# A pipelined attention and feed-forward kernel on one core: rotary tables renewed in two halves, the norm's mean computed by another instruction, and ScalarE's value copy moved in two of every four steps

## The chip, the cores and the metric

The kernel runs on one core of one Trainium2 chip. The metric is the device time of one execution in microseconds, the median over several runs. Before the change three runs gave 3952.9, 3954.86 and 3955.82 us.

## What is computed

`x` is 4 sequences of 1024 tokens of 128 channels, in float32. Two stacks of layers follow each other, each behind a layer norm and with a residual around it: eight blocks of linear attention with a feed-forward part, and then six layers of windowed attention with a feed-forward part. The change touches the second stack only (cut from the reference):

```
for i in range(DEPTH):                       # 6
    x = attn_layer(shift_tokens(x), Wqkv[i], q_scale[i], k_scale[i], Wo[i]) + x
    x = ffn_layer(shift_tokens(x), ln_g[i], ln_b[i], W1[i], b1[i], W2[i], b2[i]) + x
# attn_layer, 16 heads of 64:
q = l2norm(q) * qs;  k = l2norm(k) * ksc
q = q * cos * scale + rotate_half(q) * sin * scale
k = k * cos * inv + rotate_half(k) * sin * inv
out = local_attention(q, k, v)               # windows of 32, each sees itself and the one before
# ffn_layer:
mu = x.mean(-1, keepdims=True);  var = ((x - mu) ** 2).mean(-1, keepdims=True)
xn = (x - mu) / jnp.sqrt(var + 1e-05) * g + bln
a, gate = jnp.split(xn @ W1 + b1, 2, -1);  out = a * gelu(gate) @ W2 + b2
```

## The kernel before, in words

The program is written engine by engine: one loop over steps for each engine, in an order fixed by hand, with semaphores between them. Nothing schedules it afterwards. The first stack takes the first fifth of the time. The second works on tiles of 128 tokens: 6 layers of NT = 32 tiles are 192 tiles, and step `s` of every engine's loop holds pieces of several tiles. The products of tile s+1 are made, its squares and rotations taken (`square`, `sin_k`, `cos_k`, `sin_q`, `cos_q`, `sumsq`), tile s is turned and scored (`turned_k`, `turned_q`, `values`, `scores`, `masked`, `maxima`), tile s-1 goes through the exponentials (`exponents`, 16 heads, four at a time, one ScalarE instruction each), tile s-2 or s-3 through the attention product and the output.

The feed-forward part works on chunks of 4 tiles, so its pieces come round every four steps, and the steps differ by `s` mod 4. The text calls them:

- **turn step** (s mod 4 = 0, `stage(s, 8)`): the chunk is turned on TensorE, its mean and variance are taken on VectorE (`ff_stats`), rstd on GpSimd (`ff_rstd`), and ScalarE scales it (`ff_unit`, L980).
- **back step** (1, `stage(s, 9)`): turned back, ScalarE applies gain and bias (`ff_norm`, L988).
- **gate step** (2, `stage(s, 10)`): gates, values, gelu (`ff_gelu`, L994) and VectorE's `ff_hidden` (L1298).
- **down step** (3, `stage(s, 11)`): the second product and `ff_final` (L1305).

Lines that the text speaks of:

- ScalarE: L947 `turned_k` copies the turned keys, one in each step, and so marks the steps in the trace; L960 `exponents`; L952 `turned_q`; L975 `values` copies the value product out of PSUM and signals `v_r`; L936 `square`; L968 `outputs`.
- TensorE: L671 `product`, four matmuls, three times in a step (keys of tile s+1, queries of s+1, values of s); L724 `scores`; L743 `attend`; L703 turns. `keys_of` shares the two PSUM banks of the value product, and waits for `v_r` of the value copy:

```
                if t >= 2:
                    pe.wait_ge(v_r, t - 1)
```

- VectorE: L1185 `table_of` makes, for one tile position, the product of the rotary tables with the layer's scales (both in SBUF), 128x256 elements; it runs for the 8 positions of a sequence at the end of 8 steps before a new layer, 40 times in all. L1141 `tables_of` does it once for layer 0, in four instructions of 128x512. L1189 and L1196 (`cos`, `sin`) read these tables. L1217 `sumsq`. L1292 and L1293 in `ff_stats` write the negated mean and the variance plus epsilon. L1260 `masked` waits for all 16 exponentials of the tile before (`exp_r`), since it rewrites what they read. L1275 `turn_probs` transposes the probabilities; the next tile's exponentials wait for it (`pt_r`).
- GpSimd: L463 `add_k`, L468 `add_q`, L479 and L485 (`unit_k`, `unit_q`), L472 `probs_norm`, and L491 and L493 in `ff_rstd`; all read SBUF. Its order in a step: ff_rstd, add_q, unit_k, probs_norm, unit_q, add_k.

Of the kernel before, what the change touches and what calls it, by code (L numbers as in the profile page):

```python
# [14 lines left out]
ALU = mybir.AluOpType  # L15
# [4 lines left out]
P = 128  # L20
# [3 lines left out]
LAYERS, HEADS, DH, WIN = 6, 16, 64, 32  # L24
# [8 lines left out]
TS = SEQ // P  # L33
NT = NB * TS
# [9 lines left out]
EPS_PRE, EPS_A, EPS_F, EPS_Z = 1e-5, 1e-6, 1e-5, 1e-6  # L44
# [16 lines left out]
B_SC = B_WO + NP * D  # L61
# [10 lines left out]
def build(nc, xT, wa1, wa2, wb, wf, rot, mask, outT):  # L72
    with ExitStack() as ctx:
        def sb(name, shape):
            return ctx.enter_context(nc.sbuf_tensor(name, shape, F32))

        def sem(name):
            return ctx.enter_context(nc.semaphore(name))
# [13 lines left out]
        WB = sb("WB", [P, B_W])  # L92
# [3 lines left out]
        rotary = sb("rotary", [P, 4, TS, DH])  # L96
        tables = sb("tables", [P, 4, TS, DH])
# [4 lines left out]
        mv = sb("mv", [P, UT, 4, 2])  # L102
        ve = sb("ve", [P, UT, 4])
        rstd = sb("rstd", [P, UT, 4])
        mneg, shift = sb("mneg", [P, 4]), sb("shift", [P, 4])
# [17 lines left out]
        def carve(sizes):  # L123
# [32 lines left out]
        lq, lk, lv, lo, ls, lf = (sem(k) for k in ("wq_in", "wk_in", "wv_in", "wo_in", "scales_in", "wf_in"))  # L156
# [17 lines left out]
        fx_in, ft_mm, fst_r, frs_r, fn_r, fb_mm, xn_r, g_mm, a_mm, gate_r, hf_r, o_mm, fin_r = (sem(k) for k in (  # L174
            "ff_in", "ff_turned", "ff_stats", "ff_rstd", "ff_unit", "ff_back", "ff_normed", "gate_mm", "value_mm",
            "gate_ready", "hidden_ready", "ff_out", "ff_done"))
# [27 lines left out]
        def live(t):  # L204

            return 0 <= t < TILES

        def chunk(s, lag):

            return (s - lag) // PER if (s - lag) % PER == 0 and 0 <= s - lag < TILES else None  # L210

        def stage(s, lag):

            q = chunk(s + 1, lag)
            return q if q == FF - 1 else chunk(s, lag) if chunk(s, lag) != FF - 1 else None
# [29 lines left out]
        def heads(ap):  # L245
            return ap.rearrange("p (h d) -> p h d", d=DH)
# [597 lines left out]
        def _(act):  # L844
# [45 lines left out]
            def ff_gelu(c):  # L890
                act.wait_ge(f2_mm, MA * c + 4)
                act.activation(g2[c % 2], ps[:, F2_BANK, :], ACT.Gelu_apprx_tanh, bias=vec(c, A2_BF2))\
                    .then_inc(g2_r, 1)
# [39 lines left out]
            def square(t, src, half, mm, count):  # L933
                act.wait_ge(mm, t + 1)
                need(act, red_r, t)
                act.activation(sq[:, half], src.rearrange("p b c -> p (b c)"), ACT.Square).then_inc(count, 1)  # L936
# [7 lines left out]
            def turned_k(t):  # L944
                act.wait_ge(trk_mm, t + 1)
                act.wait_ge(shift_r, t + 1)
                act.activation(kT[:, :, WIN:WIN + P], s_ps.rearrange("p b (c t) -> p (b c) t", t=P),  # L947
                               ACT.Copy).then_inc(kT_r, 1)

            def turned_q(t):  # L950
                act.wait_ge(trq_mm, t + 1)
                act.activation(qTf, s_ps.rearrange("p b c -> p (b c)"), ACT.Copy).then_inc(qT_r, 1)  # L952

            def exponents(t, some):

                if some[0] == 0:
                    act.wait_ge(max_r, t + 1)
                    need(act, pt_r, t)
                for h in some:
                    i = act.activation(pe3[:, :, h, :], sc[:, 64 * h:64 * h + 64].rearrange("p (k q) -> p k q", k=2),  # L960
                                       ACT.Exp, bias=nmx[:, h:h + 1], accum_out=rs[:, h:h + 1])
                if some[-1] == HEADS - 1:
                    i.then_inc(exp_r, 1)

            def outputs(t):
                act.wait_ge(pv_mm, t + 1)
                need(act, wo_r, t)
                act.activation(OTf.rearrange("p (c r q) -> p r c q", r=2, q=WIN),  # L968
                               o_ps.rearrange("p r (c q) -> p r c q", q=WIN), ACT.Copy).then_inc(ot_r, 1)
# [28 lines left out]
            for s in range(-3, TILES + LAG):  # L998
                if live(s + 1):
                    square(s + 1, kv_ps, K, k_mm, sqk_r)  # L1000
                if live(s - 3):
                    outputs(s - 3)
                if live(s + 1):
                    square(s + 1, q_ps, Q, q_mm, sqq_r)
                if live(s):
                    turned_k(s)
                if live(s - 1):
                    exponents(s - 1, range(0, 4))
                    exponents(s - 1, range(4, 8))
                if live(s):  # L1010
                    turned_q(s)
                if live(s - 1):
                    exponents(s - 1, range(8, 12))
                if stage(s, 10) is not None:
                    ff_gelu(stage(s, 10), 0)
                    ff_gelu(stage(s, 10), 1)
                if live(s):
                    values(s)
                if stage(s, 9) is not None:
                    ff_norm(stage(s, 9))  # L1020
                if stage(s, 8) is not None:
                    ff_unit(stage(s, 8))
                if stage(s, 10) is not None:
                    ff_gelu(stage(s, 10), 2)
                if live(s - 1):
                    exponents(s - 1, range(12, 16))
                if 0 < s + 1 < TILES:
                    keys_on(s + 1)
# [3 lines left out]
        def _(dve):  # L1032
# [144 lines left out]
                    dve.wait_ge(loaded, 48)  # L1177
                    tables_of(0)

            def table_of(t):  # L1180

                if t % NT == 0:
                    dve.wait_ge(ls, 16 * (t // NT + 1))
                scales = WB[:, B_SC:B_SC + 4 * DH].rearrange("p (i d) -> p i d", i=4)
                dve.tensor_tensor(tables[:, :, t % TS, :], rotary[:, :, t % TS, :], scales, ALU.mult).then_inc(tab_r, 1)  # L1185

            def cos(t, src, half, o, count):
                w = tables[:, o, t % TS:t % TS + 1, :].to_broadcast([P, HEADS, DH])
# [27 lines left out]
            def sumsq(t):  # L1216
                dve.tensor_reduce(ssq[:, :], heads(sq), AX_X, ALU.add).then_inc(red_r, 1)  # L1217
# [64 lines left out]
            def ff_stats(q):  # L1282
                dve.wait_ge(ft_mm, q + 1)
                for j in range(PER):
                    o = dve.bn_stats(stats[:, 0, j, :], ps[:, FO_BANK(q), j * P:(j + 1) * P])
                o.then_inc(fst_r, 1)
                dve.wait_ge(fst_r, 3 * q + 1)
                for j in range(PER):
                    o = dve.bn_aggr(mv[:, 0, j, :], stats[:, 0, j, :])
                o.then_inc(fst_r, 1)  # L1290
                dve.wait_ge(fst_r, 3 * q + 2)
                dve.tensor_scalar(mneg[:, :], mv[:, 0, :, 0], -1.0, None, ALU.mult)  # L1292
                dve.tensor_scalar(ve[:, 0, :], mv[:, 0, :, 1], EPS_F, None, ALU.add).then_inc(fst_r, 1)  # L1293

            def ff_hidden(q, m):
                dve.wait_ge(gate_r, MF * q + m + 1)
# [18 lines left out]
            for s in range(-3, TILES + LAG):  # L1315
                if s > 0 and live(s + 1) and (s + 1) % NT == 0:
                    dve.wait_ge(tab_r, 4 + TS * ((s + 1) // NT))
                if live(s + 1):
                    sin_k(s + 1)
                if live(s - 2):  # L1320
                    turn_probs(s - 2)
                if live(s + 1):
                    cos_k(s + 1)
                if stage(s, 8) is not None:
                    ff_stats(stage(s, 8))
                if live(s + 1):
                    sin_q(s + 1)
                    cos_q(s + 1)
                    sumsq(s + 1)
                if stage(s, 10) is not None:  # L1330
                    ff_hidden(stage(s, 10), 0)
                if stage(s, 11) is not None:
                    ff_final(stage(s, 11))
                if stage(s, 10) is not None:
                    ff_hidden(stage(s, 10), 1)
                if live(s - 3):
                    residual(s - 3)
                if live(s + 1):
                    norms(s + 1)
                if stage(s, 10) is not None:  # L1340
                    ff_hidden(stage(s, 10), 2)
                if live(s):
                    masked(s)
                if live(s - 1):
                    inverse(s - 1)
                if live(s):
                    maxima(s)
                if live(s + 1 + TS) and (s + 1 + TS) // NT > (s + 1) // NT and s >= -1:
                    table_of(s + 1 + TS)
                q = stage(s, 12)  # L1350
                if q is not None and q >= FF - NT // PER:
                    final(q)
# [71 lines left out]
```

## Time and profile before

| | |
|---|---|
| median of 3 runs | 3954.86 us |
| the profiled execution, its own time | 3945.2 us |
| its span, first to last instruction | 3943.3 us |
| mean granted TensorE clock | 0.985 |
| PE (TensorE) busy | 3714.9 us, 94% |
| DVE (VectorE) busy | 3453.9 us, 88% |
| ACT (ScalarE) busy | 3279.6 us, 83% |
| POOL (GpSimd) busy | 2401.3 us, 61% |

The profile is one execution. Times in the trace are microseconds from the span's start. An engine's idle time before an instruction is put down to what released it; "issue" is time for which the profile shows no releaser.

### The profile page before, as it was taken

The page shows a single profiled execution, that of the slowest core. Times are in us where ns is not written, and L with a number is a line of the kernel's source. Part 1 is how long each engine was busy: PE and PEld are TensorE (multiplying, and loading weights), DVE is VectorE, ACT ScalarE, POOL GpSimd, SP SyncE. Part 2 cuts the span into 40 slices and gives each one's busy share as a digit, 9 for nine tenths or more (in the row PEclk, how much of TensorE's full clock was granted, in tenths as well). Part 3 has the DMA queues.
Part 4 walks back from the last instruction along what each step waited for, and adds up shares of the span by engine and source line. Part 5 has one row for each costly group of instructions (what it writes and reads, how often), then busy time and mean ns, then how long its engine had stood idle before and what let it go on. Part 6 is the DMA issues. An engine that isn't in the chain of part 4 may idle for free.

```text
span 3943.3 us, 124130 instructions
## 1 busy us (share of the span) xinstructions
PE 3714.9 (94%) x49248; PEld 2335.7 (59%) x49248; DVE 3453.9 (88%) x7052; ACT 3279.6 (83%) x9259; POOL 2401.3 (61%) x1476
## 2 busy tenths in 40 slices
PE   6999999978999999999999999999999999999997
PEld 3444444445666666666666666666666666666664
DVE  7999999968889898889989899898988989888894
ACT  4999999956888788888888888888888888888885
POOL 2444444447767676766767666676666766676672
PEclk8999999989999999999999999999999999999998
DMA  1000001002223233232232233332323223232222
GB/s 38 9 9 9 9 9 50 1 3 61 82 82 87 77 87 83 81 92 81 82 85 81 82 85 88 83 83 80 87 81 85 81 79 95 80 85 82 79 81 57
DMA packets 129889, 263.10 MB, mean 67 GB/s; under 512 B 34976, under 2 KB 36768, under 8 KB 129056
## 3 DMA queue, kind: packets, MB, share of 16 engines
q1 hardware_dynamic: 129312, 255.16, 23.1%
q8 instruction: 392, 6.42, 0.7%
q14 instruction: 185, 1.52, 0.1%
HBM read 26.43 MB, written 2.10 MB: 7 GB/s over the span
## 4 chain that ended last, share of the span: by engine, by line
PE 42%; DVE 24%; ACT 20%; issue 7%; POOL 3%; DMA 1%; SPq 1%; ACTq 0%; DVEq 0%; POOLq 0%
ACT arena L960 10%; PE ps L671 9%; PE ps L608 6%; PE ps L603 5%; PE ps L743 4%; PE ps L547 4%; DVE arena L1196 4%; DVE arena L1189 3%; DVE arena L1275 3%; PE ps L515 3%; DVE ssq L1217 3%; DVE arena L1260 2%; ACT arena L952 2%; ACT arena L947 2%; PE ps L791 2%
## 5 line engine op out<-in xcount | busy, mean ns | idle before, releaser
L960 ACT ACTIVATE arena<-arena,nmx 128x64 f32<-128x64 f32 x3072 | 1024.3, 339 | 55.3 <-DVE arena L1275 53.0
L479 POOL TENSOR_TENSOR arena<-arena,rinv 128x1024 f32<-128x1024 f32 x192 | 365.6, 1904 | 615.1 <-DVE rinv L1248 615.1
L671 PE MATMUL ps<-WB,arena 128*128 128x512 f32 x1152 | 566.9, 615 | 35.1 <-ACT arena L975 28.4
L671 PE MATMUL ps<-WN,arena 128*128 128x512 f32 x1152 | 562.4, 611 | 34.5 <-ACT arena L975 29.3
L960 ACT ACTIVATION_READ_ACCUMULATOR arena<-arena,nmx 128x1 f32 x3072 | 589.6, 192 | 0.0
L936 ACT ACTIVATE arena<-ps 128x1024 f32<-128x1024 f32 x384 | 392.2, 1022 | 227.0 <-PE ps L671 221.6
L463 POOL TENSOR_TENSOR arena<-arena 128x1024 f32<-128x1024 f32 x192 | 454.2, 2366 | 193.7 <-DVE arena L1189 178.4
L1196 DVE TENSOR_TENSOR arena<-ps,tables 128x512 f32<-128x512 f32 x768 | 489.9, 677 | 17.0 <-ACT arena L936 16.6
L468 POOL TENSOR_TENSOR arena<-arena 128x1024 f32<-128x1024 f32 x192 | 453.9, 2364 | 51.0 <-DVE arena L1189 46.9
L743 PEld LDWEIGHTS ps<-arena 128*64 128x64 f32 x12288 | 377.0, 138 | 164.9 <-issue 139.0
L1189 DVE TENSOR_TENSOR arena<-ps,tables 128x1024 f32<-128x1024 f32 x384 | 459.0, 1195 | 0.0
L1217 DVE TENSOR_REDUCE ssq<-arena 128x32 f32<-128x2048 f32 x192 | 435.0, 2266 | 0.0
L703 PEld LDWEIGHTS ps<-ident,arena 128*128 128x128 f32 x3072 | 354.1, 142 | 121.4 <-issue 98.8
L743 PE MATMUL ps<-arena 128*64 128x64 f32 x12288 | 402.6, 224 | 16.9 <-DMA arena<-arena 11.6
L472 POOL TENSOR_TENSOR arena<-arena,rr 128x1024 f32<-128x1024 f32 x192 | 368.0, 1917 | 82.3 <-DVE rr L1269 82.1
L703 PE MATMUL ps<-ident,arena 128*128 128x128 f32 x3072 | 401.8, 274 | 15.6 <-POOL arena L485 5.5
L724 PEld LDWEIGHTS ps<-arena 64*32 64x32 f32 x24576 | 266.1, 105 | 201.4 <-issue 199.0
L752 PE MATMUL ps<-arena,WB 128*128 128x128 f32 x3072 | 377.3, 276 | 1.4 <-ACT arena L968 1.1
L485 POOL TENSOR_TENSOR arena<-arena,rinv 128x1024 f32<-128x1024 f32 x192 | 375.2, 1954 | 0.0
L752 PEld LDWEIGHTS ps<-arena,WB 128*128 128x128 f32 x3072 | 360.8, 193 | 1.8 <-ACT arena L968 1.3
L420 POOL TENSOR_TENSOR rstdA<-veA,power 128x4 f32<-128x4 f32 x128 | 129.7, 1013 | 374.7 <-DVE veA L1135 374.7
L724 PE MATMUL ps<-arena 64*32 64x64 f32 x24576 | 300.1, 225 | 47.0 <-issue 24.1
(111 smaller groups left out, 7040.7 us busy)
## 6 DMA issues: line engine op xcount, KB each, us to landing
arena<-arena SPq DMA_DIRECT2D x1536, 64.0 KB, 2.0
arena<-arena SPq DMA_DIRECT2D x192, 384.0 KB, 3.4
arena<-arena SPq DMA_DIRECT2D x192, 128.0 KB, 3.5
arena<-X SPq DMA_DIRECT2D x96, 128.0 KB, 3.0
arena<-Y SPq DMA_DIRECT2D x96, 128.0 KB, 3.1
WB<-wb SPq DMA_DIRECT2D x15, 512.0 KB, 5.1
arena<-wa SPq DMA_DIRECT2D x8, 581.0 KB, 4.1
WN<-wb SPq DMA_DIRECT2D x9, 512.0 KB, 5.0
```

Source lines behind the costliest of these rows:

```text
L463: pool.tensor_tensor(tu[:, K], t1[:, K], t2[:, K], ALU.add).then_inc(addk_r, 1)
L468: pool.tensor_tensor(tu[:, Q], t1[:, Q], t2[:, Q], ALU.add).then_inc(addq_r, 1)
L671: i = pe.matmul(banks[:, c, :], x, W[:, w * INNER + c * COL:w * INNER + (c + 1) * COL], start=True, stop=True)
L703: i = pe.transpose(s_ps[:, j // 4, (j % 4) * P:(j % 4 + 1) * P], src[:, j * P:(j + 1) * P], ident[:, :])
L724: i = pe.matmul(s_ps[WIN * w:WIN * (w + 1), a, c * 64:c * 64 + 64], qT[r, c, WIN * w:WIN * (w + 1)], kT[r, c, WIN * w:WIN * (w + 2)], star ...
L743: i = pe.matmul(o_ps[64 * a:64 * a + 64, side, c * 64:(c + 1) * 64], vv[t % RING][:, side, h * DH:(h + 1) * DH], pw[:, side, :, a, c, :], ...
L752: i = pe.matmul(o_ps[:, 0, 0:P], WB[:, B_WO + c * D:B_WO + (c + 1) * D], OT[:, c, :], start=(c == 0), stop=(c == NP - 1))
L936: act.activation(sq[:, half], src.rearrange("p b c -> p (b c)"), ACT.Square).then_inc(count, 1)
L960: i = act.activation(pe3[:, :, h, :], sc[:, 64 * h:64 * h + 64].rearrange("p (k q) -> p k q", k=2), ACT.Exp, bias=nmx[:, h:h + 1], accum_o ...
L1189: dve.tensor_tensor(heads(t1[:, half]), src.rearrange("p b (h d) -> p (b h) d", d=DH), w, ALU.mult)\
L1196: k = dve.tensor_tensor(heads(t2[:, half])[:, :, here], src.rearrange("p b (h d) -> p (b h) d", d=DH)[:, :, there], w, ALU.mult)
L1217: dve.tensor_reduce(ssq[:, :], heads(sq), AX_X, ALU.add).then_inc(red_r, 1)
```

## The change

Three edits, the constants and all data unchanged.

```
@@ scalar engine, step s
                 if live(s):
                     turned_q(s)
+                early = stage(s, 8) is not None or stage(s, 9) is not None
+                if live(s) and early:
+                    values(s)
                 if live(s - 1):
                     exponents(s - 1, range(8, 12))
                 if stage(s, 10) is not None:
                     ff_gelu(stage(s, 10), 0)
                     ff_gelu(stage(s, 10), 1)
-                if live(s):
+                if live(s) and not early:
                     values(s)
@@ vector engine
-            def table_of(t):
-
-                if t % NT == 0:
-                    dve.wait_ge(ls, 16 * (t // NT + 1))
-                scales = WB[:, B_SC:B_SC + 4 * DH].rearrange("p (i d) -> p i d", i=4)
-                dve.tensor_tensor(tables[:, :, t % TS, :], rotary[:, :, t % TS, :], scales, ALU.mult).then_inc(tab_r, 1)
+            def tables_half(l, half, t):
+
+                dve.wait_ge(ls, 16 * (l + 1))
+                dve.wait_ge(rotq_r, 2 * (t + 1))
+                some = slice(TS // 2 * half, TS // 2 * (half + 1))
+                for i in range(4):
+                    w = WB[:, B_SC + i * DH:B_SC + (i + 1) * DH].unsqueeze(1).to_broadcast([P, TS // 2, DH])
+                    dve.tensor_tensor(tables[:, i, some, :], rotary[:, i, some, :], w, ALU.mult).then_inc(tab_r, 1)
@@ ff_stats
-                dve.tensor_scalar(mneg[:, :], mv[:, 0, :, 0], -1.0, None, ALU.mult)
-                dve.tensor_scalar(ve[:, 0, :], mv[:, 0, :, 1], EPS_F, None, ALU.add).then_inc(fst_r, 1)
+                mean, var = mv[:, 0, :, 0], mv[:, 0, :, 1]
+                dve.scalar_tensor_tensor(mneg[:, :], mean, -2.0, mean, ALU.mult, ALU.add)
+                dve.scalar_tensor_tensor(ve[:, 0, :], var, EPS_F, var, ALU.add, ALU.max).then_inc(fst_r, 1)
@@ vector engine, step s, behind sumsq(s + 1)
+                l = (s + 1) // NT + 1
+                if s > 0 and l < LAYERS and (s + 1) % NT in (NT - 5, NT - 1):
+                    tables_half(l, (s + 1) % NT == NT - 1, s + 1)
@@ vector engine, step s, behind maxima(s)
-                if live(s + 1 + TS) and (s + 1 + TS) // NT > (s + 1) // NT and s >= -1:
-                    table_of(s + 1 + TS)
```

The order on ScalarE, a back step before the change (arena is the one large SBUF tensor that holds most buffers, ps is PSUM, WF the feed-forward weights):

```order
L947 ACTIVATE arena<-ps 128x8x128
L960 ACTIVATE arena,rs<-arena,nmx 128x2x32 x8
L952 ACTIVATE arena<-ps 128x1024
L960 ACTIVATE arena,rs<-arena,nmx 128x2x32 x4
L975 ACTIVATE arena<-ps 128x1024
L988 ACTIVATE arena<-ps,WF 128x512
L960 ACTIVATE arena,rs<-arena,nmx 128x2x32 x4
```

The same on ScalarE with the change:

```order
L947 ACTIVATE arena<-ps 128x8x128
L960 ACTIVATE arena,rs<-arena,nmx 128x2x32 x8
L952 ACTIVATE arena<-ps 128x1024
L975 ACTIVATE arena<-ps 128x1024
L960 ACTIVATE arena,rs<-arena,nmx 128x2x32 x4
L988 ACTIVATE arena<-ps,WF 128x512
L960 ACTIVATE arena,rs<-arena,nmx 128x2x32 x4
```

The value copy (L975) now stands ahead of the third four exponentials; in turn steps it is the same with L980 in place of L988, and gate and down steps keep their order.

The order on VectorE before, from the end of one of the 40 steps with a table to its next rotations:

```order
L1260 TENSOR_TENSOR arena<-ps,maskt 128x1024
L1269 RECIPROCAL rr<-rs 128x16
L1265 TENSOR_REDUCE nmx<-arena 128x16
L1185 TENSOR_TENSOR tables<-rotary,WB 128x4x64
L1196 TENSOR_TENSOR arena<-ps,tables 128x16x32 x2
L1275 STREAM_TRANSPOSE arena<-arena 128x1024
```

And on VectorE with the change, in one of the 10 gate steps that now renew half of the tables (L1194 is `cos_q`, L1222 `sumsq`, L1304 `ff_hidden`, L1285 `residual`, L1226 `clamp`, by the new line numbers):

```order
L1194 TENSOR_TENSOR arena<-ps,tables 128x1024
L1222 TENSOR_REDUCE ssq<-arena 128x32
L1190 TENSOR_TENSOR tables<-rotary,WB 128x256 x4
L1304 SCALAR_TENSOR_TENSOR arena<-ps,WF,arena 128x512 x2
L1285 TENSOR_TENSOR Y<-ps,X 128x128
L1226 TENSOR_SCALAR ssc<-ssq 128x32
```

The table products left the end of eight consecutive steps and stand, four together, between `sumsq` and `ff_hidden` of two gate steps in each layer. TensorE's, GpSimd's and SyncE's orders are unchanged.

## Rows read from the trace of the kernel before

**Rows 1.** Page: busy us of each engine, share of the span, instructions.

```profile
PE 3714.9 (94%) x49248; PEld 2335.7 (59%) x49248; DVE 3453.9 (88%) x7052; ACT 3279.6 (83%) x9259; POOL 2401.3 (61%) x1476
```

**Rows 2.** Chain of waits in order of time: start us, us, what. A turn step.

```profile
2020.30 0.92 ACT arena L975
...
2021.35 1.95 PE ps L671 x4
```

**Rows 3.** Waits: engine and line, what released it, us in total, times, longest.

```profile
DVE arena L1298 <- ACT arena L994: 137.1, 81, 3.2
...
PE ps L671 <- ACT arena L975: 57.7, 89, 0.8
```

**Rows 4.** Timeline of a turn step: start us, us, engine, line, [idle before <-releaser].

```profile
2014.96 2.37 POOL L463 TENSOR_TENSOR arena<-arena 128x1024 f32<-128x1024 f32 x1 [0.61 <-DVE arena L1189]
...
2016.14 1.21 DVE L1292 TENSOR_SCALAR mneg<-mv 128x4 f32<-128x4 f32 x1
...
2017.26 1.88 PE L671 MATMUL ps<-WB,arena 128*128 128x512 f32 x4
...
2017.97 1.00 ACT L952 ACTIVATE arena<-ps 128x1024 f32<-128x1024 f32 x1
...
2023.71 0.21 ACT L960 ACTIVATION_READ_ACCUMULATOR arena<-arena,nmx 128x1 f32 x1
...
2024.02 1.23 DVE L1260 TENSOR_TENSOR arena<-ps,maskt 128x1024 f32<-128x1024 f32 x1
...
2027.91 1.25 DVE L1275 STREAM_TRANSPOSE arena<-arena 128x1024 f32<-128x1024 f32 x1 [0.22 <-POOL arena L472]
...
2029.25 0.35 ACT L960 ACTIVATE arena<-arena,nmx 128x64 f32<-128x64 f32 x1
```

**Rows 5.** Timeline of the back step that follows.

```profile
2031.04 1.88 PE L671 MATMUL ps<-WB,arena 128*128 128x512 f32 x4
...
2031.92 1.00 ACT L952 ACTIVATE arena<-ps 128x1024 f32<-128x1024 f32 x1
...
2033.07 1.59 PE L724 MATMUL ps<-arena 64*32 64x64 f32 x128
...
2035.30 1.96 PE L671 MATMUL ps<-WB,arena 128*128 128x512 f32 x4 [0.65 <-ACT arena L975]
...
2036.95 0.19 ACT L960 ACTIVATION_READ_ACCUMULATOR arena<-arena,nmx 128x1 f32 x1
...
2042.15 1.02 ACT L947 ACTIVATE arena<-ps 128x1024 f32<-128x1024 f32 x1
```

**Rows 6.** Timeline of the gate step that follows.

```profile
2045.44 2.27 DVE L1217 TENSOR_REDUCE ssq<-arena 128x32 f32<-128x2048 f32 x1
...
2045.60 2.37 POOL L468 TENSOR_TENSOR arena<-arena 128x1024 f32<-128x1024 f32 x1
...
2050.06 0.75 DVE L1298 SCALAR_TENSOR_TENSOR arena<-ps,WF,arena 128x512 f32<-128x512 f32 x1 [2.36 <-ACT arena L994]
```

**Rows 7.** Groups of instructions: line, engine, shapes, count, busy us, mean ns, idle before.

```profile
L1185 DVE TENSOR_TENSOR tables<-rotary,WB 128x256 f32<-128x256 f32 x40 | 62.1, 1553 | 0.0
L1292 DVE TENSOR_SCALAR mneg<-mv 128x4 f32<-128x4 f32 x48 | 53.4, 1113 | 1.7
...
L1134 DVE TENSOR_SCALAR mnegA<-mvA 128x4 f32<-128x4 f32 x128 | 21.8, 170 | 4.4
```

**Rows 8.** One line's instructions: count, ns least/median/most, first and last start.

```profile
L1141 DVE TENSOR_TENSOR tables<-rotary,WB x4: 677/678/1687, 838.1 to 840.9; 128x512 f32<-128x512 f32 x4
```

**Rows 9.** One line's instructions, the first squaring of the root steps.

```profile
L1236 DVE TENSOR_TENSOR nwt<-rinv x192: 191/192/2371, 897.0 to 3868.9; 128x32 f32<-128x32 f32 x192
```

**Rows 10.** Timeline of L947: starts of steps 47, 55 and 63.

```profile
1624.23 1.02 ACT L947 ACTIVATE arena<-ps 128x1024 f32<-128x1024 f32 x1
...
1746.37 1.02 ACT L947 ACTIVATE arena<-ps 128x1024 f32<-128x1024 f32 x1
...
1875.51 1.02 ACT L947 ACTIVATE arena<-ps 128x1024 f32<-128x1024 f32 x1
```

## The prediction

> **What bounds the kernel now.** I read four views. The page first [rows 1]: TensorE is busy 94% of the span, VectorE 88%, ScalarE 83%; no engine has much air, and an average over steps of four kinds does not say which one sets the end. So next the chain of waits, in order of time [rows 2]: what to see there is a hand-over in the turn step, where ScalarE's value copy L975 ends and TensorE's key products L671 start. Then the waits [rows 3]: TensorE stood 57.7 us before L671 for that copy, in 89 steps, never above 0.8 us; and VectorE stood 137.1 us before L1298 for the gelus, 2.9 us for each of the 48 chunks, all in gate steps. Last the timelines of a turn, a back and a gate step [rows 4 to 6], from which the arithmetic is made.
>
> A loop over two engines limits a step besides TensorE. The last exponential of a tile ends at 2023.92 (L960 at 2023.71, [rows 4]), `masked` L1260 can start 0.1 us later, then follow the reciprocal, `maxima`, `sin_k` and the transpose L1275, and only when that has ended, at 2029.16, may the next tile's exponentials begin: they do at 2029.25. So in the turn step this loop and not TensorE releases ScalarE.
>
> **1. Tables.** Removed: 40 instructions L1185 of 1553 ns, 62.1 us [rows 7]. Each stands at a step's end, in that loop, between `maxima` and `sin_k`. What they cost the end is read from the step marks: from step 47 to 55 no table is made, 122.14 us; from 55 to 63 the eight tables of a layer are made, 129.14 us [rows 10], the same eight kinds of steps. That is 7.0 us for eight, of 12.4 us of instructions. For five layer changes: 35 us gained.
>
> Added: 10 times four instructions of 128x256, with the same 40 x 256 elements. Why did the old ones take 1553 ns? The same product over 512 elements took 678 ns in its median, 1687 at most [rows 8], and 4 elements take 170 ns (L1134, [rows 7]). The line through the two, 1 ns for each element, gives 0.42 us for 256; that is what I take. Bounds: 0.34 (half of 678) and 1.55 (as before). What makes the difference is GpSimd working at the same time. In the gate step `sumsq` ends at 2047.71 and GpSimd's L468 at 2047.97 [rows 6]; behind it GpSimd has nothing until VectorE's root steps. If the first instruction waits for 2047.97, four end at 2047.97 + 4 x 0.42 = 2049.65, and L1298 is to start at 2050.06, 0.65 earlier once edit 3 acts: 2049.41. Not hidden: 0.2 us, 10 times, 2 us. The new wait for `rotq_r` is for an instruction ahead of `sumsq` on the same engine, and costs nothing; behind it queue `ff_hidden` and the root steps, for which GpSimd waits. With the upper bound the four take 6.2 us, 4.5 beyond the cover left, 45 us in all: no gain from this edit but a loss of 10. Tables: 33 us gained (between +10 lost and 35 gained).
>
> **2. The mean.** L1292 writes 128x4 values and takes 1113 ns in its mean [rows 7], the same form in the first stack 170 ns (L1134). The timeline says why: it starts at 2016.14 and ends at 2017.35, when GpSimd's L463 ends, at 2017.33 [rows 4]. If the new form escapes, 48 x 0.94 = 45 us of VectorE go, all in turn steps. Does it? It now reads `mean` twice, as two SBUF inputs. The nearest row is L1236, which also takes one SBUF tensor twice: 192 ns, but 2371 once [rows 9], when it began beside GpSimd's L468. So an instruction with two SBUF inputs can be held too, and I expect L1292's successor to take about 1.1 us still.
>
> The Trainium skill ("SBUF — State Buffer", section "Who interferes with whom") says the same more sharply: a VectorE instruction with two SBUF inputs contends with a GpSimd instruction that reads SBUF, and the later one is blocked entirely. By it the edit removes nothing; that the old form is held agrees with the trace, for the new form no row of this kernel exists.
>
> Either way the sum hardly moves: L1260 starts 0.1 us after the last exponential, so a VectorE that is 1 us earlier at that point waits instead. I take 0 (between 0 and 45).
>
> **3. The value copy.** *Back step* [rows 5]: the value product ends at 2032.92, `turned_q` at 2032.92, so L975 can follow at once; its successors in PSUM, the keys, then wait only for TensorE. The scores end at 2034.66, and TensorE's keys follow at once, 0.65 us earlier than 2035.30. Behind them on TensorE stand `attend`, the queries and the turn of the keys, each without another wait that lasts as long (L988, for which `attend` waits, keeps its place behind 12 exponentials and one copy), so L947 of the next step comes at 2041.5 instead of 2042.15. The loop allows it: the last exponential keeps its end at 2037.14, and 5.11 us later (the time from 2023.92 to 2029.25, less the 0.22 us that L1275 stood for GpSimd) is 2042.25; ScalarE is ready about 0.9 us behind the start of L947 (its 1.02 us less the overlap seen between neighbours), at 2042.4. Of the 57.7 us, back steps hold the share 0.65 / (0.65 + 0.76) = 27 us.
>
> *Turn step* [rows 4]: the value product ends at 2019.14, later than `turned_q` at 2018.97. ScalarE, which goes on about 0.1 us before 2018.97 now, stands until 2019.18: 0.3 us in which the exponentials behind it would have run. They end 0.3 later, `masked` starts 0.3 later, and the 0.22 us for GpSimd before L1275 swallow most of that: 0.08 us are left. TensorE's keys come 0.76 us earlier, but the next exponentials are released by the loop, so this is not gained. Cost: 48 x 0.08 = 4 us, taken off what the back steps win, 27 - 4 = 23 us. (Bounds: 57.7 if all of the wait pays, and -14 if 0.3 us were lost in each turn step and nothing won.)
>
> **Sum.** 33 + 0 + 23 = 56 us off the profiled execution's 3945.2: 3889. The median of the runs shown is 9.7 above that execution, so the median forecast is 3899.
>
> **The rivals.**
> - *The value copy pays nothing* (0.15). For it: the loop is only 0.2 us behind in the back step, and TensorE has gaps of its own inside the scores that no reordering moves. Against: 0.65 us is a wait that ends last in 44 steps. Tables alone: 3955 - 33 = 3922.
> - *The mean escapes, and VectorE was the bound in turn steps* (0.09). Then turn steps gain as well, all of the 57.7: 3955 - 33 - 58 = 3864. Against: L1236's 2371, and L1260's place behind the exponentials.
> - *The tables are held as before* (0.06): halves at 1.55 us each, 10 us lost, 23 gained by the copy: 3942. Against: GpSimd is idle from 2047.97 on.
> - *Slower: ScalarE stands before the value copy* (0.06). The copy now has 4 exponentials behind it, which the loop needs. If the value product came as late as 1 us behind `turned_q` (in the turn step it is 0.17 behind), 96 steps would lose nearly 1 us each: 96 - 33 = 63 slower, 4018. It decides from (33 + 2)/96 = 0.36 us of lateness on. Against: in the back step it is not late at all.
> - *Nothing to be seen* (0.04): table gain given back by waits elsewhere in the 8 steps; 3955.
>
> **How the numbers follow.** The forecast has 0.60: 3899, with 3884 to 3914 for the bounds of its terms. About 0.2% (8 us) is what a measurement of this kernel can tell from no change. Faster by more: 0.60 + 0.15 + 0.09 + 0.05 of the third rival, 0.88 after rounding down; within: 0.05; slower: 0.07. The range for 8 in 10 takes in the tables-alone case and, half, the case of the mean: 3868 to 3927.
>
> **What would show it.** The table group: 40 instructions near 0.4 us, and steps 55 to 63 within 1 us of steps 47 to 55. The successor of L1292: near 1.1 us if it is held, 0.17 if it escapes. L671's wait for L975 gone in turn and back steps; back steps 0.5 us shorter or more, turn steps no shorter. VectorE's idle time before L1298 smaller by 1.6 us in ten gate steps. I am wrong if turn steps get shorter (the loop was not the bound), if L975 waits over 0.3 us for the value product, or if the halves take over 1 us each.

## The result, and the profile after

Four runs of the changed kernel gave 3901.35 us (3897.38 to 3905.21); four of the kernel before, one of them new, 3955.34 us. The ratio is 0.9871, with a 95% interval of 0.9856 to 0.9886: 1.3% less, 45 to 57 us. The profiled execution took 3905.21 us, its span 3903.4 us against 3943.3; it is the slowest of the four, so the two traces stand 40 us apart where the medians stand 54. Of all the executions below one, of the run with the mean alone, was slow (6865.9 us, at a granted clock of 0.83), and it is left out of that run's ratio.

The page of the changed kernel, busy time by engine, which answers to [rows 1]:

```profile
PE 3706.9 (95%) x49248; PEld 2330.6 (60%) x49248; DVE 3410.1 (87%) x7052; ACT 3278.4 (84%) x9259; POOL 2392.7 (61%) x1476
```

VectorE is 43.8 us less busy. Its groups of instructions, which answer to [rows 7] (line, shapes, count, busy us, mean ns, idle before):

```profile
L1298 DVE SCALAR_TENSOR_TENSOR mneg<-mv 128x4 f32<-128x4 f32 x48 | 51.8, 1078 | 1.6
...
L1190 DVE TENSOR_TENSOR tables<-rotary,WB 128x256 f32<-128x256 f32 x40 | 16.3, 464 | 0.0
```

The 40 table products went from 1553 to 464 ns each; the mean in its new form takes 1078 ns, as good as the 1113 of the old. The waits, which answer to [rows 3]:

```profile
DVE arena L1304 <- ACT arena L994: 116.0, 74, 3.2
DVE arena L1265 <- ACT arena L960: 106.2, 146, 3.2
...
PE ps L743 <- DMA arena<-arena: 38.8, 55, 6.3
```

VectorE's wait for the gelus, the cover of the tables, fell from 137.1 to 116.0 us. TensorE's wait for the value copy, 57.7 us before, is 4.3 us (6 times). The third of these lines is new in size: `attend` L743 is put down as waiting 38.8 us for DMAs, 11.6 us before. The timeline of one back step shows such a wait (start us, us, engine, line, idle before):

```profile
2391.27 1.00 ACT L952 ACTIVATE arena<-ps 128x1024 f32<-128x1024 f32 x1
2392.17 1.00 ACT L975 ACTIVATE arena<-ps 128x1024 f32<-128x1024 f32 x1
...
2394.04 1.98 PE L671 MATMUL ps<-WN,arena 128*128 128x512 f32 x4
...
2397.26 2.08 PE L743 MATMUL ps<-arena 128*64 128x64 f32 x64 [1.24 <-DMA arena<-arena]
```

The copy follows `turned_q` at once and the keys start without a wait, as forecast. But behind them `attend` stands 1.24 us. The chain of waits in order of time says for what:

```profile
2387.29 1.23 DVE arena L1280
...
2388.53 0.54 SPq L325
...
2389.12 0.59 SPq L326
...
2392.92 0.59 SPq L326
...
2394.19 3.04 DMA arena<-arena
...
2397.26 2.08 PE ps L743 x64
```

From the transpose's end at 2388.52 SyncE issues eight DMAs (`widen`, which spreads the probabilities over the wide buffer that `attend` reads), one every 0.63 us, until 2393.51; then they have to land. The last piece of the chain is named after L332, the DMA that SyncE issues next, but that one moves the values of a tile whose `attend` comes later; `attend` here waits for the last widening DMA, issued at 2392.92. From issue to landing that one took 4.2 us, where the median is 2.0:

```profile
L326 SPq DMA_DIRECT2D arena<-arena x4: 590/591/594, 2389.1 to 2392.9; - x4
...
DMA to landing us min/median/max: 2.0/2.0/4.2
```

In the trace fifteen of its sixteen parts have landed by 2394.90 and the last at 2397.12, and `attend` starts 0.14 us later. So it goes in 19 of 46 back steps (in 22 before the change): the last part lands over 1 us behind the others. Of the 20.2 us that `attend` stands in back steps, 16.1 fall in those 19. What holds the last part up isn't shown.

Not all of the 38.8 us is a wait for these DMAs. In turn steps it looks like this:

```profile
2380.77 1.48 ACT L980 ACTIVATE arena<-ps,shift,rstd 128x128 f32<-128x128 f32 x4
2382.30 1.30 PEld L743 LDWEIGHTS ps<-arena 128*64 128x64 f32 x42 [1.28 <-ACT arena L980]
2382.30 1.39 PE L743 MATMUL ps<-arena 128*64 128x64 f32 x40 [0.45 <-DMA arena<-arena]
```

`attend` starts 0.05 us behind the end of ScalarE's L980, for which it waits too, and the widening DMAs had landed about 2.8 us earlier; the line that names a DMA names the wrong one of several waits. There are 25 such stands of about 0.45 us in the row, 11 us, and all but one of the rest, 26.6 us in 29 steps, end with the last widening DMA.

Where the marks of the steps stand now:

```profile
1622.35 0.35 ACT L960 ACTIVATE arena<-arena,nmx 128x64 f32<-128x64 f32 x1
...
1743.04 0.35 ACT L960 ACTIVATE arena<-arena,nmx 128x64 f32<-128x64 f32 x1
...
1864.25 0.35 ACT L960 ACTIVATE arena<-arena,nmx 128x64 f32<-128x64 f32 x1
```

These are the first exponentials of steps 47, 55 and 63: 120.7 us without tables, 121.2 us with the two halves. The table stretch costs 0.5 us more than the one ahead of it, where it cost 8.3 before.

### The profile page after: what moved, and what is told of

It is laid out like the page before. It is cut to its first block, busy times and chain, and to the rows that moved or that the text cites. A ratio compares the mean times of both kernels' runs of the same rounds, so it can differ in the third digit from the quotient of the medians.

```text
span 3903.4 us, 124140 instructions
## 1 busy us (share of the span) xinstructions
PE 3706.9 (95%) x49248; PEld 2330.6 (60%) x49248; DVE 3410.1 (87%) x7052; ACT 3278.4 (84%) x9259; POOL 2392.7 (61%) x1476
## 4 chain that ended last, share of the span: by engine, by line
PE 66%; ACT 15%; DVE 7%; issue 5%; SPq 3%; DMA 3%; POOL 1%; ACTq 0%; DVEq 0%; POOLq 0%
PE ps L671 18%; ACT arena L960 8%; PE ps L743 8%; PE ps L608 6%; PE ps L603 5%; PE ps L752 5%; PE ps L703 5%; PE ps L547 4%; PE ps L515 3%; PE ps L724 3%; PE ps L806 3%; DMA arena<-arena 2%; PE ps L791 2%; PE ps L799 2%; SPq L325 2%
## 5 line engine op out<-in xcount | busy, mean ns | idle before, releaser
L479 POOL TENSOR_TENSOR arena<-arena,rinv 128x1024 f32<-128x1024 f32 x192 | 365.3, 1902 | 613.1 <-DVE rinv L1253 613.1
L671 PE MATMUL ps<-WB,arena 128*128 128x512 f32 x1152 | 573.6, 622 | 7.6 <-ACT arena L975 4.3
L671 PE MATMUL ps<-WN,arena 128*128 128x512 f32 x1152 | 562.6, 611 | 3.0 <-DVE arena L1194 3.0
L743 PEld LDWEIGHTS ps<-arena 128*64 128x64 f32 x12288 | 378.1, 139 | 199.8 <-issue 133.9
L468 POOL TENSOR_TENSOR arena<-arena 128x1024 f32<-128x1024 f32 x192 | 453.7, 2363 | 53.2 <-DVE arena L1194 47.5
L1194 DVE TENSOR_TENSOR arena<-ps,tables 128x1024 f32<-128x1024 f32 x384 | 459.3, 1196 | 0.0
L743 PE MATMUL ps<-arena 128*64 128x64 f32 x12288 | 404.1, 224 | 46.1 <-DMA arena<-arena 38.8
L1222 DVE TENSOR_REDUCE ssq<-arena 128x32 f32<-128x2048 f32 x192 | 435.1, 2266 | 0.0
L472 POOL TENSOR_TENSOR arena<-arena,rr 128x1024 f32<-128x1024 f32 x192 | 367.8, 1916 | 86.6 <-DVE rr L1274 86.3
L485 POOL TENSOR_TENSOR arena<-arena,rinv 128x1024 f32<-128x1024 f32 x192 | 367.7, 1915 | 0.0
```

Source lines behind the costliest of these rows:

```text
L468: pool.tensor_tensor(tu[:, Q], t1[:, Q], t2[:, Q], ALU.add).then_inc(addq_r, 1)
L671: i = pe.matmul(banks[:, c, :], x, W[:, w * INNER + c * COL:w * INNER + (c + 1) * COL], start=True, stop=True)
L743: i = pe.matmul(o_ps[64 * a:64 * a + 64, side, c * 64:(c + 1) * 64], vv[t % RING][:, side, h * DH:(h + 1) * DH], pw[:, side, :, a, c, :], ...
L1194: dve.tensor_tensor(heads(t1[:, half]), src.rearrange("p b (h d) -> p (b h) d", d=DH), w, ALU.mult)\
```

## The experiments

Each run is compared by ratio with the kernel before on the same chip; in us it is said of 3955, to stand beside 3901. The sets were run at other times and on several chips; their medians for the kernel before are 3948 to 3949, not 3955, and which of the two makes that isn't known.

A step is measured below from its first exponential to the next step's, as the median over the steps without tables. In the kernel before a turn step is 13.94 us and a back step 13.80; in the changed kernel 13.94 and 13.75.

**Each edit alone.** Tables only is the changed kernel with these lines undone:

```
-                early = stage(s, 8) is not None or stage(s, 9) is not None
+                early = False
-                dve.scalar_tensor_tensor(mneg[:, :], mean, -2.0, mean, ALU.mult, ALU.add)
-                dve.scalar_tensor_tensor(ve[:, 0, :], var, EPS_F, var, ALU.add, ALU.max).then_inc(fst_r, 1)
+                dve.tensor_scalar(mneg[:, :], mv[:, 0, :, 0], -1.0, None, ALU.mult)
+                dve.tensor_scalar(ve[:, 0, :], mv[:, 0, :, 1], EPS_F, None, ALU.add).then_inc(fst_r, 1)
```

> The changed kernel with the copy and the mean as before, so that the tables in halves stand alone. Theory (tables carry most of the gain: the first exponentials of turn, back and gate steps come 2.5, 0.5 and 1.3 us sooner in each of 10 steps with tables, about 41 us): 3915 us against 3955, and back and turn steps without tables as before. Rival (the copy carries most): the tables alone give 28 us or less, 3927 or more.

Measured: 3900.66 us, ratio 0.9887 (0.9868 to 0.9906), 45 us of gain. The tables carry most of it; the rival is out. In the profiled executions 39 of the 45 us between this kernel and the one before lie in the five stretches with tables. Their instructions take 467 ns as in the changed kernel.

Copy only is the kernel before with the first hunk of the change.

> The kernel before with only the value copy moved, in turn and back steps. Theory: the wait of L671 for L975 (57.7 us before) is gone, but TensorE's attend now waits for the widening DMAs (38.8 us in the changed kernel, 11.7 before), and turn steps stay bound by the exponentials' loop: 8 to 20 us gained, 3940. The forecast's own figure was 23 us, 3932. Rival (the copy pays all it removes): over 40 us, below 3915.

Measured: 3939.0 us, ratio 0.998 (0.9969 to 0.9992), 8 us of gain (3 to 12). The forecast's figure of 23 is out, and so is the rival. The typical turn and back step are 13.94 and 13.76 us. L671's wait for the copy is 4.3 us, and the wait for DMAs appears here too, without the other edits:

```profile
PE ps L743 <- DMA arena<-arena: 49.0, 71, 6.6
```

Mean only is the kernel before with the last two `+` lines of `ff_stats`.

> The kernel before with only the mean and the variance in the new form. Theory (two SBUF inputs are held as long as the old form, 1.08 us in the changed kernel): within 3 us of before, 3955, its group near 1.1 us in the mean. Rival (the form is worth something, by the shorter hold in some steps): 5 us or more gained.

Measured: 3948.75 us, ratio 0.9998 (0.9985 to 1.001): no effect that can be told from none.

```profile
L1293 DVE SCALAR_TENSOR_TENSOR mneg<-mv 128x4 f32<-128x4 f32 x48 | 52.9, 1102 | 1.6
```

The form is held as the old one was. The three ratios multiplied give 0.9865, the change 0.9871: as far as these intervals tell, the edits add up.

**The copy in back steps only**, with the tables and the old mean:

```
-                early = stage(s, 8) is not None or stage(s, 9) is not None
+                early = stage(s, 9) is not None
```

> The changed kernel with the copy moved in back steps only (turn steps as before) and the mean as before. Theory (the copy in turn steps delays ScalarE by 0.3 us and wins nothing, the back step alone wins): 3898, equal to the changed kernel's 3901 or 1 to 4 us faster. Rival (turn steps win too, since attend of the turn step starts 0.25 us sooner): 5 us or more slower than the changed kernel.

Measured: 3897.87 us, ratio 0.9874 (0.9856 to 0.9892), not to be told from the change's 0.9871. So the copy's move in turn steps is worth nothing that could be seen, as forecast (the forecast had it lose 4 us, which is below the noise).

**Half of the widening DMAs left out**, with the change and then with the tables alone. In `widen` (the counts that three waits ask for go down with it):

```
                     sp.dma_start(PTw[q, w % 2, here], pt[q, COL:2 * COL]).then_inc(wide_in, 16)
-                    sp.dma_start(PTw[o:o + WIN, w % 2, here], pt[q, 0:COL]).then_inc(wide_in, 16)
```

> The changed kernel with four of the eight widening DMAs of each tile left out (those of the window before are not brought into the wide buffer, so the attention product leaves them out), and its waits counted accordingly. Theory (attend waits for these DMAs since the keys come sooner, 38.8 us in 55 steps, and that is where the copy's gain went): that wait falls below 5 us and the time falls by 10 to 25 us below the changed kernel's 3901, to about 3885. Rival (the exponentials' loop takes the gain anyway): the wait goes, the time stays within 5 us of 3901.

> The tables in halves alone (value copy and mean as before), with the same four of eight widening DMAs left out: the control to the run with the copy. Theory (the DMAs matter only where the copy lets the keys come sooner, since the wait was 11.9 us in 12 steps without it): at most 10 us below the tables alone, 3890 to 3900, and so the copy is worth 15 us or more once the DMAs are short. Rival (fewer DMAs help whatever the order is): 20 us or more below the tables alone, 3880 or less, the copy still worth 8 or less.

Measured: with the copy 3874.88 us, ratio 0.9812 (0.9798 to 0.9827); without it 3897.45 us, ratio 0.9863 (0.985 to 0.9876). With the copy the time fell by 23 us below the change. In pairs: with all DMAs the copy takes the ratio from 0.9887 to 0.9871, 6 us (-3 to 16 by the two intervals); with half of them from 0.9863 to 0.9812, 20 us (12 to 28). The difference, 14 us, is thus known to some 12 us only. The steps tell it more sharply:

| | turn step, us | back step, us |
|---|---|---|
| tables only | 13.92 | 13.79 |
| the change | 13.94 | 13.75 |
| half of the DMAs, no copy | 13.93 | 13.79 |
| half of the DMAs, with the copy | 13.94 | 12.99 |

With all eight DMAs the copy's move leaves the typical back step as it was, with four it takes 0.8 us off it. Neither fewer DMAs alone nor the copy alone shortens it. (By ratio the run with half of the DMAs and no copy is 9 us below tables only, at the edge of what the intervals tell.) The 0.8 us would be 38 us in 48 back steps; the medians of the runs give 20, and where the rest goes isn't shown. The row of `attend` in the run with the copy:

```profile
PE ps L742 <- DMA arena<-arena: 12.5, 27, 0.6
```

That is not below 5, as was expected, but none of it is a wait for widening DMAs: all 27 are turn steps, where `attend` follows ScalarE's L979 (L980 elsewhere) and the widening DMAs landed some 5 us earlier. In back steps they land 3.4 us before `attend` starts, with no last part behind the others by more than 1 us.

**One exponential ahead of the copy in turn steps:**

```
+                lead = 1 if stage(s, 8) is not None else 0
+                if live(s - 1) and lead:
+                    exponents(s - 1, range(8, 8 + lead))
                 if live(s) and early:
                     values(s)
                 if live(s - 1):
-                    exponents(s - 1, range(8, 12))
+                    exponents(s - 1, range(8 + lead, 12))
```

> The changed kernel with one more head's exponential ahead of the value copy in turn steps, so that ScalarE does not stand 0.3 us for the value product. Theory (the loop from the last exponential to the next first one sets the turn step, and the stand is in it): turn steps 0.3 us shorter from first exponential to first exponential, 48 times, up to 14 us, 3890. Rival (something else, TensorE's attend behind L980 or the DMAs, sets the turn step): within 4 us of 3901.

Measured: 3896.06 us, ratio 0.9877 (0.9859 to 0.9894): not to be told from the change, where the theory's 14 us would have given 0.984. The timeline of a turn step tells why:

```profile
1454.36 1.22 DVE L1268 TENSOR_TENSOR arena<-ps,maskt 128x1024 f32<-128x1024 f32 x1
...
1458.24 1.25 DVE L1283 STREAM_TRANSPOSE arena<-arena 128x1024 f32<-128x1024 f32 x1 [0.21 <-POOL arena L472]
...
1454.43 1.90 POOL L479 TENSOR_TENSOR arena<-arena,rinv 128x1024 f32<-128x1024 f32 x1 [1.92 <-DVE rinv L1256]
1456.30 1.92 POOL L472 TENSOR_TENSOR arena<-arena,rr 128x1024 f32<-128x1024 f32 x1
```

Counted from the first exponential, the last one ends at 8.60 us (8.92 in the changed kernel) and `masked` starts at 8.70 (9.02), but the transpose starts at 12.58 (12.61): it now waits 0.21 us for GpSimd's L472, which stands behind L479, which waited for VectorE's root steps. The turn step is 13.93 us in its median, 13.94 in the changed kernel: a second chain, through the root steps and GpSimd, is as long as the first.

**The mean by a reduction.** First one of the two instructions, then both:

```
-                dve.scalar_tensor_tensor(mneg[:, :], mean, -2.0, mean, ALU.mult, ALU.add)
+                dve.tensor_reduce(mneg[:, :], mv[:, 0, :, 0:1], AX_X, ALU.max, negate=True)
...
+                dve.tensor_reduce(ve[:, 0, :], mv[:, 0, :, 1:2], AX_X, ALU.max).then_inc(fst_r, 1)
```

> The changed kernel with the negated mean written by a reduction over one element, one SBUF input, with the variance in its old form. Theory: this form is not held by GpSimd, its group falls from 1.08 us to under 0.25, VectorE is 0.8 us earlier in turn steps and then waits for ScalarE's last exponential, so the time stays within 4 us of 3901. Rival (VectorE's hold is worth time): 10 us or more gained. If the group stays near 1.1 us the hold is not a matter of the second input.

Measured: 3902.73 us, ratio 0.9881 (0.9865 to 0.9896). The reduction takes 157 ns, but the tensor_scalar behind it then takes the hold over:

```profile
L1298 DVE TENSOR_SCALAR ve<-mv 128x4 f32<-128x4 f32 x48 | 49.4, 1030 | 0.0
...
L1297 DVE TENSOR_REDUCE mneg<-mv 128x4 f32<-128x4 f32 x48 | 7.5, 157 | 1.6
```

VectorE was hardly sooner free, so this run says which form is held, not what the hold costs.

> The changed kernel with the negated mean and the variance both written by a reduction over one element, so that neither has a second SBUF input nor is a tensor_scalar; the epsilon is left out of the variance. In the run with one reduction the reduction took 157 ns and the tensor_scalar behind it 1030. Theory: both take under 0.2 us, VectorE waits longer for ScalarE's last exponential instead, the time within 5 us of 3901. Rival (VectorE's hold is worth time): 10 us or more gained.

Measured: 3884.48 us, ratio 0.9832 (0.9815 to 0.9848): 15 us below the change, with intervals that do not meet. So the theory's "within 5" is out, and the rival's number came. A turn step of this run:

```profile
1440.73 0.16 DVE L1297 TENSOR_REDUCE mneg<-mv 128x4 f32<-128x4 f32 x1
1440.81 0.15 DVE L1298 TENSOR_REDUCE ve<-mv 128x4 f32<-128x4 f32 x1
...
1448.93 1.23 DVE L1265 TENSOR_TENSOR arena<-ps,maskt 128x1024 f32<-128x1024 f32 x1 [1.35 <-ACT arena L960]
```

VectorE is 1 us earlier and waits that 1 us before `masked`: 1.36 us in its median, 0.32 in the changed kernel. The typical turn step is 13.94 us in both. So the theory holds for the typical step, and the gain isn't in it. TensorE stands now and then within the scores, 1 to 2.5 us with no releaser:

```profile
2088.95 0.30 PE L724 MATMUL ps<-arena 64*32 64x64 f32 x3 [2.38 <-issue]
2089.17 3.66 PE L671 MATMUL ps<-WB,arena 128*128 128x512 f32 x4
```

(These two lines are from the changed kernel.) Such stands over 0.8 us make 23.0 us in the changed kernel's trace (11 of them), and the nine groups of four matmuls that took over 2.5 us, where 1.95 is usual, another 13.6; with both reductions they are 12.3 us (6) and 2.2 (two groups). That is 22 of the 26 us between the two profiled executions, but these are single executions, one of them the slowest of its four; the other traces, all with the hold, have 14 to 23 us of such stands. Whether the missing hold has a part in there being fewer, or is worth time in some other way in the untypical steps, isn't settled: no run here changes the stands alone.

**The halves in the old place:** behind `maxima` in place of behind `sumsq`, in the same gate steps.

```
-                if s > 0 and l < LAYERS and (s + 1) % NT in (NT - 5, NT - 1):
-                    tables_half(l, (s + 1) % NT == NT - 1, s + 1)
...
                 if live(s):
                     maxima(s)
+                l = (s + 1) // NT + 1
+                if s > 0 and l < LAYERS and (s + 1) % NT in (NT - 5, NT - 1):
+                    tables_half(l, (s + 1) % NT == NT - 1, s + 1)
```

> The changed kernel with the halves behind the maxima of the same gate steps, where the old products stood, beside GpSimd's L472 and L485. Theory (the old products were slow because of their place, held by GpSimd): four take 4 to 6 us, in the exponentials' loop, 10 times 3 to 5 us in full: 3931 to 3951, most of the tables' gain lost. Rival (the form, four contiguous halves, is what made them fast): each stays near 0.46 us, 10 x 1.7 = 17 us lost, 3918.

Measured: 3942.34 us, ratio 0.9984 (0.9975 to 0.9993): 45 us slower than the change, the tables' gain given back whole.

```profile
L1190 DVE TENSOR_TENSOR tables<-rotary,WB 128x256 f32<-128x256 f32 x40 | 39.7, 1050 | 0.0
```

1050 ns is a mean of two kinds. One set of four, and GpSimd beside it:

```profile
1307.81 3.98 DVE L1190 TENSOR_TENSOR tables<-rotary,WB 128x256 f32<-128x256 f32 x4
...
1306.87 1.92 POOL L472 TENSOR_TENSOR arena<-arena,rr 128x1024 f32<-128x1024 f32 x1 [1.33 <-DVE rr L1274]
1308.74 2.08 POOL L485 TENSOR_TENSOR arena<-arena,rinv 128x1024 f32<-128x1024 f32 x1
```

The first two take 1.26 and 2.12 us and each ends 0.3 us behind GpSimd's L472 and L485; the last two, with GpSimd done, take 0.41 each. Behind `sumsq` the first takes 0.6, with the end of L468 beside it, and the other three 0.41. So the place makes them slow or fast and not the form: the old ones, 1.26 to 1.84 us, had GpSimd beside all of them. The four are 4 us in one piece, in the loop, 10 times: 40 us.

**Two versions against the DMA chain.** Two of the eight DMAs issued by GpSimd behind its second unit product (it is `widen`'s w = 3, with a semaphore of its own):

```
+                if live(s - 2):
+                    widen_last(s - 2)
                 if live(s + 1):
                     add_k(s + 1)
```

> The changed kernel with two of the eight widening DMAs issued by GpSimd, behind its second unit product, and six by SyncE, whose issue chain is 1.3 us shorter. Theory (attend waits for the last widening DMA): the wait of L743 for DMAs falls below 15 us and the time by 8 to 20 us, 3885. Rival (issuing them costs GpSimd more than its idle 0.6 us, or they land late): the same or slower than 3901.

Measured: 3892.23 us, ratio 0.9852 (0.9839 to 0.9866). `attend`'s wait for DMAs is put at 16.7 us, a little over what was expected, but none of it in back steps (the last tile apart): there the last widening DMA lands 2.1 us before `attend` starts. The time is 8 us below the change, with intervals that overlap (0.9856 to 0.9886). The back step fell to 13.30 us and the turn step rose to 14.33: most of what one wins the other gives back. Which of the products behind the two issues on GpSimd (0.58 and 0.50 us) makes the turn step longer isn't shown.

```
-                dve.transpose(pt, pe_).then_inc(pt_r, 1)
+                for k in (1, 0):
+                    dve.transpose(pt[:, k * COL:(k + 1) * COL], pe_[:, k * COL:(k + 1) * COL]).then_inc(pt_r, 1)
```

Here SyncE issues the four DMAs of the first half after the first transpose.

> The changed kernel with the transpose of the probabilities in two halves, so that the first four widening DMAs start 0.6 us sooner. Theory (the DMA chain bounds attend, VectorE's loop pays 0.07 us a step for the second instruction, 13 us at most): between 3885 and 3900. Rival (the loop pays more than the chain wins): 3905 to 3915.

Measured: 3893.27 us, ratio 0.9852 (0.9839 to 0.9866), the wait 28.4 us. Here too the back step is shorter, 13.28 us, and the turn step longer, 14.11. These two have the lowest ratios of the kernels that leave nothing out, but neither is set apart from the change with certainty.

## Why the prediction was right, and where it was not

The forecast was 3899 us, the measured 3901.35. That the sum came out so close is luck: two of its terms were wrong, and their errors, +12 and -15, stood against each other.

*Tables: 33 forecast, 45 measured (37 to 52), above the term's own upper bound of 35.* The mechanism was right: the new place is free of GpSimd's hold but for the end of L468 (0.42 us forecast for an instruction, 0.41 measured where GpSimd is idle, 0.464 in the mean; 1.05 in the old place), and it is covered by the wait for the gelus. The size was read at the wrong mark. The forecast took 7.0 us for eight tables from the starts of L947 [rows 10]. But the last table of the eight stands at the end of step 62, and delays the transpose and the exponentials of step 63, which start behind L947 of that step. The first exponentials of the same steps in the trace before:

```profile
1625.27 0.35 ACT L960 ACTIVATE arena<-arena,nmx 128x64 f32<-128x64 f32 x1
...
1747.40 0.35 ACT L960 ACTIVATE arena<-arena,nmx 128x64 f32<-128x64 f32 x1
...
1877.85 0.35 ACT L960 ACTIVATE arena<-arena,nmx 128x64 f32<-128x64 f32 x1 [1.32 <-DVE arena L1275]
```

130.45 against 122.13 us, 8.3 for this layer change. Over all five the stretches with tables are longer than those ahead of them by 42.8 us between first exponentials and by 35.9 between L947. The forecast had itself named that loop as the place. Nor did the halves cost the 2 us that were put down for them: in a gate step that has them L1304 still waits for the gelu.

```profile
1365.22 1.64 DVE L1190 TENSOR_TENSOR tables<-rotary,WB 128x256 f32<-128x256 f32 x4
1367.60 0.75 DVE L1304 SCALAR_TENSOR_TENSOR arena<-ps,WF,arena 128x512 f32<-128x512 f32 x1 [0.74 <-ACT arena L994]
```

*The value copy: 23 forecast, 8 measured alone (3 to 12), 6 on top of the tables (-3 to 16).* The step that failed is "each without another wait that lasts as long", of what stands behind the keys. `attend` had such a wait: for the widening DMAs. It hardly showed before (3.7 us in all back steps), since the last of these DMAs landed just before `attend` could start, 0.4 us in the median; with keys 0.65 us sooner it ends last. The forecast looked for such a wait on ScalarE (L988) and not on SyncE, whose eight issues are 5 us from the transpose's end, with a last part that in 19 of 46 back steps lands over 1 us late. Its sign "back steps 0.5 us shorter or more" did not come: 13.75 us for 13.80. With half of these DMAs left out the back step is 0.8 us shorter and the copy is worth 20 us (12 to 28), which takes in the 23.

*Turn steps win nothing:* right, the run with the copy in back steps only shows it. Of the reason, half: besides the loop of the exponentials there is the chain through root steps and GpSimd's L472, of equal length. ScalarE stood 0.21 us for the value product, of the 0.3 forecast. By the marks of L947 the turn step did get 0.28 us shorter (13.50 for 13.78), which the forecast had named as a sign against it, and the back step as much longer (14.32 for 14.02): only the mark between them moved. From first to first exponential the turn step stayed (13.94 in both).

*The mean: held, and 0:* right for the form as changed. L1236, a tensor_tensor with one tensor twice, was the right row. The Trainium skill ("SBUF — State Buffer", section "Who interferes with whom") lets a VectorE instruction with two SBUF inputs be blocked by a GpSimd instruction that reads SBUF, and says of a reduction that it never contends. The traces agree: in this place the scalar_tensor_tensor took 1.08 to 1.10 us and the reduction 0.157. The tensor_scalar, with one SBUF input, took 1.03 to 1.11, so it was held as well. That the sum would not move if the hold went was argued from the typical step and is true of that step; the run without any hold is 15 us faster all the same. Most of what its one trace shows of that are fewer stands of TensorE, and the cause is open.

Of the rivals, "the value copy pays nothing" came nearest to what was found: with the forecast's 33 for the tables it gives 3922, which is out, but with the 45 measured it gives 3910, and the change as a whole (45 to 57 us) hardly rules that out. It is the copy alone, 3 to 12 us, that does.

## What to carry to other kernels

Read what an instruction costs between two marks that lie behind it in the loop that it delays, not at the nearest convenient mark. When a wait is taken away, list for each instruction behind it every semaphore that it waits for, with the time at which each comes, the DMA issuer's queue included: the wait that ended just before the one removed shows almost nothing in the totals and is the next bound. Where an instruction waits for several things, a profile's row names one of them: check it against when the others came, as with the 0.45 us in turn steps that a DMA was named for and ScalarE's L980 made. Keep a VectorE product of two SBUF tensors away from GpSimd's work by its place: one of 128x256 cost 0.41 us where GpSimd was idle and 1.26 to 2.12 beside it. And a sum that comes out is no proof of its terms; the runs with one edit each are what showed these two wrong.

## What was not expected of the hardware

The hold passes on: with the mean written by a reduction (0.157 us) the tensor_scalar behind it took 1.03 us, so that taking one instruction out of the hold gained VectorE next to nothing.

TensorE's stands within the scores come in the same steps in most of the 14 traces (12, 24, 25, 64, 77, 116, 129, 168, 181, each in 8 to 13 of them, with 52 steps between many). What makes them isn't known. Behind one of them the products of the keys ran at a lower clock: in the changed kernel the granted clock from 2089.1 to 2092.8 was 0.54 of full speed, nearer to 1.2 than to 2.4 GHz, and the four matmuls took 3.66 us where they take 1.9 to 2.0. The engine had stood 2.38 us before it. The windows (us, busy us and instructions of each engine, PEclk):

```profile
2080.00:2088.00 8.00, 6.14 (x155) 4.72 (x154) 7.83 (x13) 7.68 (x31) 6.24 (x3) 1.00 0.28 68
2089.10:2092.80 3.70, 3.70 (x9) 1.10 (x6) 2.48 (x3) 0.51 (x1) 3.70 (x3) 0.54 0.30 99
```

One thing is left untried: one exponential ahead of the copy in turn steps together with a mean that is not held. Each of the two chains of the turn step was shortened alone, by 0.3 us and by 1 us, and neither shortened the step; both at once were not run.
